# Early blocks in two stages through two quarters of the expert weights, with new orders of work

## The reference, cut to what matters

```python
x = layernorm(x + attention(x))                     # 16 heads share one score matrix, rank 64
# context experts: token id // 3125 picks e; Wg = Wu = Wd = ctx[e], 256 x 256
x = layernorm(x + (silu(x @ Wg[e].T) * (x @ Wu[e].T)) @ Wd[e])
# routed network: 4 experts of width 1024, the best one of softmax(x @ Wr + br)
p = softmax(x @ Wr + br); e = argmax(p)
x = layernorm(x + p[e] * ((silu(x @ Wg[e]) * (x @ Wu[e])) @ Wd[e]))
```

## Time and profile before

| | |
|---|---|
| median of 3 runs | 195.0 us (195.0 to 196.93) |
| the profiled execution's own time | 196.24 us |
| its span, first to last instruction | 194.3 us |
| TensorE busy | 176.0 us (91%) |
| VectorE busy | 132.0 us (68%) |
| ScalarE busy | 103.3 us (53%) |
| GpSimd busy | 103.0 us (53%) |
| mean granted TensorE clock | 0.980 of full |
| moved by DMA | 29.14 MB |

### The profile page before, as it was taken

The page is one execution under the profiler, slowest core; times in us unless marked ns, Lnnn a source line. Parts: engine busy times, 40 slices in busy tenths (PEclk is TensorE's granted clock), DMA queues, the critical chain, the costliest instruction groups (busy, mean ns, idle before and its releaser), DMA issues.

```text
span 194.3 us, 3905 instructions
## 1 busy us (share of the span) xinstructions
PE 176.0 (91%) x969; PEld 140.0 (72%) x969; DVE 132.0 (68%) x406; ACT 103.3 (53%) x274; POOL 103.0 (53%) x130
## 2 busy tenths in 40 slices
PE   1999997999999898989999999999999999999810
PEld 0677775447888655668888788888888888888610
DVE  3269996895678887536554454444799986888950
ACT  3136776725567935537664946643665422455530
POOL 7006356770126884627772168860588810377683
PEclk9999999999999999999999999999999999999975
DMA  5999999246999223146544105444050000011010
GB/s 157 359 336 418 378 366 319 73 139 168 322 334 405 101 85 94 29 130 173 221 149 150 46 0 165 164 162 167 0 162 3 0 0 3 0 57 56 22 62 24
DMA packets 15317, 29.14 MB, mean 150 GB/s; under 512 B 1726, under 2 KB 11968, under 8 KB 15170
## 3 DMA queue, kind: packets, MB, share of 16 engines
q1 hardware_dynamic: 13568, 25.68, 39.4%
q0 software_dynamic: 1440, 3.22, 4.7%
q10 hardware_dynamic: 290, 0.01, 0.1%
HBM read 20.41 MB, written 9.28 MB: 153 GB/s over the span
## 4 chain that ended last, share of the span: by engine, by line
PE 68%; POOL 11%; issue 7%; DMA 5%; DVE 3%; ACT 3%; POOLq 1%; SPq 1%; DVEq 0%; ACTq 0%
PE bank L484 14%; PE bank L486 13%; PE bank L485 13%; POOL out_tokens L473 5%; PE bank L729 4%; PE bank L563 4%; PE bank L652 3%; PE bank L629 3%; POOL rstd L395 3%; DMA arena<-in_attn_w 3%; PE bank L594 2%; PE bank L572 2%; PE bank L511 2%; DMA x_sorted<-buf,slot 1%; PE bank L498 1%
## 5 line engine op out<-in xcount | busy, mean ns | idle before, releaser
L391 POOL TENSOR_TENSOR w_lo<-stage,w_hi 128x512 fp32r<-128x512 f32 x40 | 51.4, 1305 | 44.0 <-ACT w_hi L803 44.0
L912 ACT ACTIVATE gate<-bank 128x256 f32<-128x256 f32 x44 | 17.0, 387 | 48.5 <-PE bank L486 48.5
L1206 DVE TENSOR_TENSOR hid<-bank,gate 128x256 f32<-128x256 f32 x44 | 18.7, 425 | 30.5 <-ACT gate L912 30.2
L484 PE MATMUL bank<-w_hi,xr 128*128 x88 | 35.9, 408 | 1.4 <-DVE xr L1164 0.8
L486 PE MATMUL bank<-w_hi,xr 128*128 x88 | 34.7, 395 | 0.0
L485 PE MATMUL bank<-w_lo,xr 128*128 x88 | 34.7, 394 | 0.0
L484 PE MATMUL bank<-w_hi,hT 128*128 x88 | 28.5, 324 | 0.7 <-DVE hT L1211 0.7
L803 ACT ACTIVATE w_hi<-stage 128x512 fp32r<-128x512 f32 x48 | 28.6, 630 | 0.3 <-PE bank L486 0.3
L486 PE MATMUL bank<-w_hi,hT 128*128 x88 | 24.9, 282 | 0.0
L485 PE MATMUL bank<-w_lo,hT 128*128 x88 | 24.8, 282 | 0.0
L484 PEld LDWEIGHTS bank<-w_hi,xr 128*128 128x128 f32 x88 | 16.6, 189 | 4.4 <-issue 2.3
(11 more groups left out here) (182 smaller groups left out, 329.7 us busy)
## 6 DMA issues: line engine op xcount, KB each, us to landing
stage<-in_w_ffn SPq DMA_DIRECT2D x16, 768.0 KB, 4.5
rows<-x_sorted SPq DMA_DIRECT2D x22, 132.0 KB, 2.3
x_sorted<-padrow SPq DMA_DIRECT2D x1, 2244.0 KB, 10.2
x_sorted<-padrow SPq DMA_DIRECT2D x1, 2112.0 KB, 16.4
buf<-in_x_tok SPq DMA_DIRECT2D x1, 1024.0 KB, 11.0
w_hi<-in_ctx SPq DMA_DIRECT2D x1, 1024.0 KB, 11.5
w_hi<-in_ctxT SPq DMA_DIRECT2D x1, 1024.0 KB, 14.0
x_sorted<-padrow SPq DMA_DIRECT2D x1, 792.0 KB, 12.7
```

The source lines that it names most:

```text
L391: g.tensor_tensor(out=lo, in0=src, in1=hi.bitcast(F32), op=ALU.subtract).then_inc(split_lo, 1)
L484: mm(dst, xhi, whi, start=start, stop=False)
L912: a(gate[:, (T + j) % 2, :], fA[j % 2][:, 0:FQ], ACT.Silu).then_inc(silu_done, 1)
L1206: v.tensor_tensor(out=hid[:, (T + j) % 2, :], in0=fA[j % 2][:, FQ:2 * FQ], in1=gate[:, (T + j) % 2, :], op=ALU.mult).then_inc(h_done, 1)
```

## The change

1. **Memory.** The context weights move out of `w_hi` into the arena, where the attention's inputs were (`ctx_f`), and `ctxn` into the down parts of the second quarter. Chunks 0 to 7 are loaded straight into `w_lo` (`load_direct`), where the rest then overwrites them in place; only chunks 8 to 15 use `stage`.
2. **Transfers.** SP's queue ahead of the first sort is: chunks 0 to 5, pads, then (after the attention's last `z_of`) the context, chunks 6 and 7. After the rows of stage 0 come chunks 8 to 10, ahead of the rows of stages 1 and 2.
3. **Splits ahead.** The 12 pieces of quarter 1 are split during the context experts, by written-out places on each engine; the last piece of each chunk comes at the end (k = 20 to 23), after `ctxn` was read. VectorE takes 17 rests in all, four of them in quarter 2.
4. **Stages.** Routed blocks 0 and 1 need context blocks 0 to 4, block 2 needs 0 to 6, the others all (`STAGE_ENDS`, `STAGE_BLOCKS`). There are three tables in place of two, and three scatter semaphores.
5. **Items.** The first six are (0,0), (0,1), (1,0), (1,1), (0,2), (1,2); then quarter 0 and quarter 1 of blocks 3 to 10, then quarters 2 and 3. For the three early blocks quarters 0 and 1 are added up in PSUM (`OPENS`, `CLOSES`).
6. **Orders.** All five engines' orders from the context experts to item 13 are written out call by call. The 21 products on constants after the context experts are gone.

```diff
-ROUTED = 7
+STAGE_ENDS = (5, 7, T)
+STAGE_BLOCKS = ((0, 2), (2, 3), (3, T))
...
+EARLY_ITEMS = [(0, 0), (0, 1), (1, 0), (1, 1), (0, 2), (1, 2)]
+ITEMS = EARLY_ITEMS + [(q, t) for q in (0, 1) for t in range(3, T)] + [(q, t) for q in (2, 3) for t in range(T)]
...
+WRITTEN_OUT = 14
+OPENS = (0, 1, 4)
+CLOSES = {2: 0, 3: 1, 5: 4}
...
+LO_BY_DVE = (4, 5, 6, 7, 8, 9, 10, 14, 15, 18, 19, 21, 22, 26, 29, 32, 35)
...
+        SHARE = {q: s for q, s in ((2, [2, 2, 2, 2, 2, 2]), (3, [0, 1, 1, 2, 1, 2, 1, 2, 1, 1, 0]))}
...
```

SP's queue:

```diff
+            def load_direct(n):
+                o = n * CHUNK
+                sp.dma_start(w_lo[:, o:o + CHUNK].bitcast(F32), wffn_in[n]).then_inc(d_direct[n], 16)
...
-            load_chunk(2)
-            sp.dma_start(ctx4[:, :, :, E:E + D], ctx_in.rearrange("p (e k d) -> p e k d", e=E, k=DK)).then_inc(d_ctx, 16)
-            load_chunk(3)
+            for n in range(2, E + 2):
+                load_direct(n)
             pads2 = scr2.rearrange("(p r) c -> p r c", p=P)
             HALF2 = BLOCKS2 // 2
             sp.dma_start(pads2[:, 0:HALF2, :], padrow[:].unsqueeze(1).broadcast_to([P, HALF2, ROW])).then_inc(d_init2, 16)
+            sp.wait_ge(z_done, BATCH)
+            sp.dma_start(ctx4[:, :, :, E:E + D], ctx_in.rearrange("p (e k d) -> p e k d", e=E, k=DK)).then_inc(d_ctx, 16)
+            load_direct(E + 2)
+            load_direct(E + 3)
...
-            for n in range(E, E + SLOTS):
-                load_chunk(n)
...
+            for s, (a, b) in enumerate(STAGE_BLOCKS):
+                sp.wait_ge(row_table, s + 1)
+                r = {t: first_row(t) for t in range(a, min(b, a + 2))}
+                begin = STAGE_ENDS[s - 1] if s else 0
+                sp.wait_ge(d_scat2[s], 16 * (STAGE_ENDS[s] - begin))
+                for t in range(a, b):
+                    if t not in r:
+                        r[t] = first_row(t)
+                    routed_row(t, r[t])
+                if s == 0:
+                    for n in range(2 * E, 2 * E + SLOTS):
+                        load_chunk(n)
...
```

GpSimd's order:

```diff
+            pool.wait_ge(split_lo_dve, 7)
+            split(11)
+            split(12)
+            split(13)
             validity()
+            split(16)
+            split(17)
+            split(20)
             root2(0)
+            split(23)
             root2(1)
             pool.wait_ge(d_init2, 32)
+            scatter2(0)
+            scatter2(1)
+            scatter2(2)
             root2(2)
+            scatter2(3)
+            scatter2(4)
             root2(3)
+            scatter2(5)
+            scatter2(6)
             root2(4)
...
```

TensorE's order from the turn of block 8's rows:

```diff
+            tx(8)
+            rank(0)
+            up(7)
+            th(6)
+            down(5)
+            tx(9)
+            up(8)
+            th(7)
+            down(6)
+            tx(10)
+            rank(1)
+            up(9)
+            th(8)
+            down(7)
+            up(10)
+            th(9)
+            down(8)
+            th(10)
+            rank(2)
+            add(9)
+            down(9)
+            add(10)
+            down(10)
             ftx(0)
+            ftx(1)
+            fup(0)
+            rank(3)
+            fup(1)
+            fth(0)
+            fup(2)
+            ftx(2)
             rank(4)
+            fth(1)
+            fdown(0)
+            fup(3)
...
+            fup(5)
+            fth(4)
+            ftx(3)
+            fdown(3)
+            ftx(4)
+            fup(6)
...
```

ScalarE's order in the middle of the context experts:

```diff
+            x1copy(5)
+            silu(4)
+            h1copy(3)
+            split(20)
+            split(21)
+            split(22)
+            x1copy(6)
+            silu(5)
+            h1copy(4)
+            x1copy(7)
+            split(23)
+            silu(6)
+            shift2(0)
+            norm2(0)
+            h1copy(5)
+            norm2(1)
...
```

VectorE's order:

```diff
+            split(10)
+            hidden(0)
+            hidden(1)
+            hidden(2)
+            split(14)
+            split(15)
+            split(18)
+            split(19)
+            hidden(3)
...
+            residual(3)
+            choose(0)
+            hidden(6)
+            residual(4)
+            split(21)
+            place(0)
+            hidden(7)
+            residual(5)
+            choose(1)
+            hidden(8)
+            residual(6)
+            place(1)
+            tables_a()
+            residual(7)
+            hidden(9)
+            choose(2)
+            hidden(10)
+            residual(8)
+            place(2)
+            tables_b()
+            residual(9)
+            fxlo(0)
+            choose(3)
+            fxlo(1)
+            residual(10)
+            place(3)
+            fhidden(0)
+            split(22)
+            choose(4)
+            fhidden(1)
+            fhlo(0)
+            place(4)
...
+            def tables_a():
+                whole_blocks(T + 2, GROUP_OF[STAGE_ENDS[0] - 1] + 1)
+                running(nth[:], whole[:])
+                row_tables(*STAGE_BLOCKS[0])
+                chosen(0, 2)
```

616 lines of the change are left out of this document (370 added, 246 removed).

## The result

The changed kernel takes **211.0 us** (median of 4 runs, 209.42 to 212.84) against 195.37 us (195.0 to 196.93): **ratio 1.0755, 95% interval 1.071 to 1.08**. The forecast was 193.7 us, its range ended at 196.8. The profiled execution, the slowest of the four, took 212.84 us with a span of 211.1, so its starts lie about 1 us further behind those of the kernel before than the medians do.

A forecast was written before the change was run, and what follows sets the result against it. TensorE was taken to bound the kernel, with all that can be won between 70 and 92 us. Terms of -0.4 and +1.7 made it 1.3 us faster, 193.7 us from the median 195.0; range 190.3 to 196.8.

The forecast's parts named there:

- Step 1, the load queue: First sort: four more chunks ahead of the sorted rows delay their first turn by 1.6 us, between 0 and 3.3.
- late-sort rival: First sort lands 3.3 us later, choose(0) and all behind it 1.4 us later, 195.1 us in all; chance 0.17.
- clock rival: TensorE's clock falls after a 3.3 us pause for the first sorted rows: 2.5 us lost, 197.6 us in all; chance 0.19.
- Step 2, splits ahead: Context experts: twelve splits moved ahead; GpSimd's root and split 23 put choose(0)'s end at 60.7 us against 57.48.
- Split 23 over choose(0): Before the context experts' hidden(6): a VectorE choose(0) operation waits out GpSimd's split, 1.3 us.
- Step 3, tables and orders: Late context experts: VectorE's added table and split set the pace; first expert product at 76.5 against 76.11, 0.4 us lost.
- Step 4, six blocks cover the second sort: fup(0) to fup(6): six early items cover the late rows with 0.5 us to spare, 13.8 us against 15.9, 1.7 won.
- it lands at 80 to 81.5: I take 0: Block 2's routed row, behind chunks 8 to 10 and scatter 6, lands in time for fup(2) and costs nothing.
- Step 5, the rest: Middle quarters: moved splits and saved copies change nothing; if the cover fails, some 0.5 us per item.
- the signs that the prediction named for being wrong: Early choose(0) or fup(0), first turn at 45.8, clock below 1.00, hole before ftx(2) or ftx(3), stall in middle quarters.

The follow-up runs named there:

- experiment 12: Changed kernel with the second quarter's four early weight chunks cut to 64 of 1536 columns, the rest zeros: ratio 1.056 to the kernel before.
- experiment 3: Changed kernel with the rests of pieces 16 and 17 made by VectorE instead of GpSimd: ratio 1.0707 to the kernel before.
- experiment 4: Changed kernel with 15 products on constants put into the wait ahead of the first turn of sorted rows: ratio 1.0622 to the kernel before.
- 7: Changed kernel: half the pads later, chunks 8-10 last, splits 16/17 on VectorE, old middle orders, VectorE's tables, TensorE's ranks and ftx(1) later: ratio 1.0521.
- 10: Changed kernel: half the pads later, chunks 8-10 last, splits 16/17 on VectorE, old middle orders, group 2's shift later, root earlier, tables and ftx(1) later: ratio 1.0477.
- experiment 2: Changed kernel with chunks 8 to 10 loaded behind all routed rows instead of behind those of blocks 0 and 1: ratio 1.058.
- experiment 18: Changed kernel: second quarter's early chunks cut to 64 columns, chunks 8-10 last, splits 16/17 on VectorE, old middle orders, shift later, 4 idle products before ftx(0): ratio 1.016.
- experiment 5: Changed kernel with fsum(9) ahead of fhidden(12) on VectorE and ScalarE's exponential ahead of fsilu(12), as in the kernel before: ratio 1.052.
- experiment 14: Changed kernel: half the pads later, chunks 8-10 last, splits 16/17 on VectorE, old middle orders, shift later, 12 idle products before ftx(0): ratio 1.0461.
- experiment 1: Changed kernel with the first half of the routed rows' pads moved behind the sorted rows: ratio 1.0575 to the kernel before.

## Why the prediction was wrong, step by step

**Step 1, the load queue: mis-sized.** It took +1.6 us at the first turn; measured +3.6 (46.12), beyond the 3.3 that it gave as its other end, and the old kernel with the same bytes +4.8. What failed is the choice between its two ends, "since the slow scatters ran beside pads, and what now fills the queue from 35 on are loads": beside loads the last two early scatters landed in 5.9 and 5.7 us instead of 2.5 and 2.4. The late-sort rival named the time of the turn (45.8) but priced it at 1.4 us; the second quarter's bytes are worth 1.95 points (experiment 12), and chunks 8 to 10 come on top (step 4).

**The clock rival (0.19) happened, and was a case of its own by mistake.** It was priced for a pause of 3.3 us; the pause was 3.17 and the clock fell from 47.4 to 50.8, then again after 3.99 us. Its price for one fall, 2.5 us, was right: filling the first wait gave back 1.3 points, 2.6 us. Here the late queue made the pause, so a forecast must carry the two together. With the queue cut the clock fell in another place (experiment 12), one of the holes that the rival had named.

**Step 2, splits ahead: right in size.** Split 23 over choose(0) cost what was said: one operation took 1.27 us. The Trainium skill ("SBUF — State Buffer", Who interferes with whom) says that a VectorE instruction with two SBUF inputs and a GpSimd one that reads SBUF exclude each other; rows and experiment 3 agree (four splits 4.70 us beside two of GpSimd, six 3.69 alone). The +2.6 us in the table is not the splits' own. From the first turn to choose(0)'s end it took 17.0 us where the clock was held (experiment 4) and 17.5 where the queue was cut (12), forecast 16.6, and VectorE's four splits behind hidden(2), put down as "nothing", took 2.49 and 2.79 us there. Only where the half clock had made hidden(2) late did they run beside GpSimd's 16 and 17, take 4.70 us, and hold hidden(3) from 52.99 to 57.62. A delay moves work on one engine beside work on another that the walk had kept apart.

**Step 3, tables and orders: only seemingly right.** choose(0) to fup(0) was put at 15.8 us and took 17.0. VectorE's part of it, to the end of fxlo(0), is 15.8 (65.30 to 81.11); behind that stand ftx(1), which shares its bank with ftx(0) and waits for fxlo(0), and 0.63 us more, 1.2 in all, for which the forecast had nothing. But where choose(0) ended at the forecast's time (experiment 12) it took 19.1 us: TensorE waited 2.02 us at rank(0), had half clock behind that, and waited 1.77 us at up(10) for a copy behind group 2's shift, whose root stands behind three scatters. The walk took VectorE as always busy there; it waited 1.25 us for TensorE at 64.25. Moving the tables won nothing (7, 10); both of these executions had 6.8 us of half clock, so the tables' own price stays open.

**Step 4, six blocks cover the second sort: right in form, but the loads were put at nothing, and little of the win lasts.** 14.06 us in experiment 2, 14.1 in 18, forecast 13.8. But item 6 then waits for a row: fup(0) to fup(7) took 18.2 and 18.1 us, before 18.5, so that 0.3 to 0.4 us are won and not 1.7. And "it lands at 80 to 81.5: I take 0" failed: the scatters in front of block 2's row shared the engines with 2.4 MB of loads and the row was issued at 88.94. The Trainium skill ("DMA: Bandwidth & Descriptors", Queues, rings and completion order) has each engine take turns between queues packet by packet. From this the prediction had concluded that a scatter beside a full queue would land soon, and had noted at the first sort that the trace disagreed; here it gave scatters beside loads no term, and two that were out by 81.5 were not done until 88.8.

**Step 5, the rest: wrong, and the largest row of the table.** "Worth nothing", "off the chain" and "made up in the next" came to 7.3 us between items 6 and 22. 3.5 of it are two orders (experiment 5): an exponential with its two table loads between two splits, and a sum behind two hiddens. 3.6 to 5.1 stay in every run with these orders mended. The price was named, 0.5 us per item, but not entered: busy time left on an engine does not cover an instruction that waits ahead of a needed one.

**The range** ended at the clock case; each rival moved one term. Five terms went the same way, since each rested on another engine or queue having room. Of the signs that the prediction named for being wrong, four came: the first turn at 45.8 or later, a clock below 1.00 between 42 and 80, a hole before ftx(2), and a stall in the middle quarters.

How the loss divides, by ratios: 1.0755; 1.056 without the second quarter's bytes; 1.016 with chunks 8 to 10 later, splits 16 and 17 on VectorE, the middle orders, the later shift and 4 products on constants too. These 4.0 points are not all orders of work: chunks 8 to 10, 1.75 points by themselves, are loads again. What is left, 1.6%, lies behind item 7 in the trace of experiment 18: against the kernel before fup(0) is 0.5 us later, fup(7) 0.1, fup(22) 3.6 and the last product 3.3. The steps don't add in any order, and the split of the 4.0 points among them is not shown.

## What to carry to other kernels

Work that is moved ahead "into idle time" must be priced at every in-order queue that it enters: what waits behind it there, and what shares its port or its DMA engines. Transfers that nobody needs soon belong behind the small ones that somebody waits for, and the wait for a late transfer can bring the clock's fall with it, which is paid as well. A gain at one point is worth only what is left of it some items later: six blocks won 1.8 us, and one item on 0.3 to 0.4 of it was left. When several small stalls are mended one at a time, expect the next wait to take most of the gain: check it on the combined kernel (6.4 points singly, 3.7 together).

## What the hardware did unexpectedly

Between 42 and 100 us the clock fell for 3.4 or for 6.8 us at a time, but not always behind the same wait. It fell behind waits of 3 to 5 us, behind one of 2.02 us in experiment 12 (60.40), and in experiment 14 from 44.8 to 48.3 behind one of 1.33 us (42.87), while it stayed up behind 2.76 us in experiment 1 (71.51) and 2.41 us in experiment 4 (87.18). Two profiled executions of nearly the same kernel can so differ by a stretch; the medians over runs carry the verdicts here, and single traces only the mechanism.

A scatter of 128 rows, which lands in 2.4 us on quiet engines, took 5.7 to 5.9 us beside the context and two loads of 768 KB on SP's queue and 7.2 to 8.3 us beside three such loads. Line L477 of the changed kernel, from 79 to 81:

```profile
DMA to landing us min/median/max: 7.2/7.7/8.3
```
